# A deep fused transformer kernel: the local attention's weights and rotary tables are loaded one stage earlier, into the buffer of the preceding cross attention

## The chip, the cores and the metric

The kernel runs as one program on one core of one Trainium2 chip. Its time is the device time of one execution in microseconds (us), and the number that counts is the median of several runs. A second execution was profiled; its rows carry the same kind of times, a little longer than an unprofiled run. Engines are named as in the profile: PE is the matmul engine (PEld its weight loads), DVE, ACT and POOL are the three elementwise engines, SP issues most of the DMA transfers.

## What is computed

The input is x of 2 x 1024 tokens with 256 channels, and a context of 2 x 64 rows with 128 channels. Four blocks follow each other, each with a gated residual around it:

```python
x = x + tanh(g_xattn[0]) * L0_xattn(layernorm(x), ctx)   # causal self attention, then cross attention, each with an MLP
x = x + tanh(g_ffn[0])   * L0_ffn(layernorm(x))          # two layers: local attention, then a gated feed-forward
x = x + tanh(g_xattn[1]) * L1_xattn(layernorm(x), ctx)   # cross attention
x = x + tanh(g_ffn[1])   * L1_ffn(layernorm(x))          # router and 16 experts
```

The change is about the second block. One of its two layers, with 8 heads of 64 and windows of 128 tokens:

```python
h = shift_token(x)                       # half of the channels come from the token before
q, k, v = split(h @ wqkv)                # 256 -> 3 x 512
q, k = l2norm(q) * q_scale, l2norm(k) * k_scale
q, k = rotary_xpos(q, k)                 # tables of cos and sin by position, times a scale
x = x + softmax(mask(8 * q @ k_window.T)) @ v_window @ wo
h = layernorm(shift_token(x)) * ln_g + ln_b
a, g = split(h @ w1 + b1)
x = x + (a * gelu(g)) @ w2 + b2
```

## The kernel before, in words

The program is a chain of stages on the same core: self attention, its tail ("t1"), cross attention ("x2"), its tail ("t2"), local attention of layer 0 ("la0"), feed-forward of layer 0 ("lf0"), "la1", "lf1", cross attention "x3", router, experts and output. Tokens lie on the 128 partitions, so there are NT = 16 tiles of 128 tokens, 8 per sequence. The residual stream lives in SBUF all the time (`xres` and `x0res`), so that no stage loads its input. Every stage is a block of its own: `signals` allocates its semaphores and has a barrier over all engines in it, then each engine runs its own list of instructions written out by hand, and `release` frees the semaphores. A stage ends when every engine, SP included, is through its list; nothing of the next stage starts before.

Most stages get their weights by an "ahead" function: the stage in front gives it to its SP list, which issues the transfers at once and waits until they have landed (`sp.wait_ge(s.next_in, ahead(sp, s.next_in))`). So x2 loads what t2 needs, and la0 what lf0 needs. The local attentions are different. `local_attention(l, ahead)` issues its own six transfers at its start on SP's queue: `wqkv` (1536 KB), two small scale vectors, the cos and the sin table and `wo` (512 KB each), and only then, on the same queue, the ten transfers of the feed-forward behind it.

The other engines of local attention start like this:

- POOL clears five small regions (the last is `maskf`, L1373), each clear counted on `built1`, and then builds the masks (L1375 to L1387).
- PE waits for `w_in` (the landing of `wqkv`) and for `built1` to be 5, and then begins with `turn_x(0)`: two transposes of the first tile (L1607). ACT copies the result to `hT` (L1565), PE projects it to queries and keys in eight matmuls (`project_qk`, L1643), and ACT squares them (`norms`, L1540). DVE sums the squares (L1466), and so on through the norm, the rotation, the scores and the softmax. `turn_x` needs no weights.
- DVE waits for `tab_in` (the landing of both tables and both scale vectors), multiplies the tables in place by the scale vectors in six instructions (L1422, L1425), and only then takes part in the chain. The first reader of the tables on DVE is `cosines` (L1494), on POOL `sines` (L1406), which waits for `tab1`.

The tail t2 (`attention_tail` with finish "gate") reads the cross attention's output `ores` ([128, 8, 1024] float32) in `project1` (L846), for four groups of four tiles; the last group is read in the middle of the stage. Afterwards nothing reads `ores`, and before the change it was freed behind t2. The feed-forwards' SP list was empty, and the third cross attention had an output buffer `ores3` of its own.

Of the kernel before, what the change touches and what calls it, by code (L numbers as in the profile page):

```python
# [9 lines left out]
def build(nc, io, out):  # L10
# [21 lines left out]
    def signals(phase, names):  # L32

        sems = []
        for n in names.split():
            sems.append(nc.alloc_semaphore(f"{phase}_{n.lstrip('@')}"))
            if not n.startswith("@"):
                nc.gpsimd.sem_inc(sems[-1], 1)  # L40
        nc.all_engine_barrier()
        return namedtuple("Signals", names.replace("@", ""))(*sems)
# [7 lines left out]
    def sb(name, shape, dt=F32, where=None):  # L50
        return (where or stack).enter_context(nc.sbuf_tensor(name, shape, dt))
# [12 lines left out]
    with stack:  # L64
# [609 lines left out]
        def attention_tail(phase, weights, out_T, finish):  # L674
# [6 lines left out]
            with ExitStack() as c:  # L681
# [18 lines left out]
                s = signals(phase, "@base_done @p1_done @x1_done @stats1 @moments1 @var1 @rstd1 @z_done @z_turned @zT_done "  # L700
                            "@h_done @gelu_done @sum1 @sum2 @p3_done @y_done @gated @stats2 @moments2 @var2 @rstd2 @scaled @x_out")
                with nc.Block() as block:
                    @block.gpsimd
# [574 lines left out]
        t2ctx = ExitStack()  # L1278
        t2_weights, t2_ahead = tail_weights("t2", "L0_xattn_a2_", t2ctx, 2 * D1)
        cross_attention("x2", H1, D1, lambda t: x0res[:, t, :], ores, x2_weights, True, None, SCALE1, t2_ahead)  # L1280
        attention_tail("t2", t2_weights, lambda t, m: ores[:, t // TPB * MC + m, t % TPB * P:(t % TPB + 1) * P], "gate")
        t2ctx.close()
        x2_ctx.close()
        attn.close()

# [6 lines left out]


        def local_attention(l, ahead):
# [8 lines left out]
            with ExitStack() as c:  # L1303
                wqkv = sb(ph + "w", [P, KD, 3, INNER], F32, c)
                wo = sb(ph + "wo", [P, INNER // P, D], F32, c)
                scl = sb(ph + "scl", [P, 2, DL], F32, c)
                cosr = sb(ph + "cos", [P, TPB, 2, DL], F32, c)
                sinr = sb(ph + "sin", [P, TPB, 2, DL], F32, c)
# [25 lines left out]
                s = signals(ph, "@next_in @wo_in @w_in @tab_in @built1 @built2 @tab1 @x_turned @h_done @qk_done "  # L1334
# [20 lines left out]
                with nc.Block() as block:  # L1355
                    @block.sync
                    def _(sp):
                        sp.dma_start(wqkv[:], io["L0_ffn_wqkv"][l].rearrange("(k p) (t n) -> p k t n", p=P, t=3)).then_inc(s.w_in, 16)
                        for n, name in enumerate(["L0_ffn_q_scale", "L0_ffn_k_scale"]):
                            sp.dma_start(scl[:, n, :], rows(io[name][l])).then_inc(s.tab_in, 16)  # L1360
                        for tab, name in ((cosr, "rotary_cos"), (sinr, "rotary_sin")):
                            sp.dma_start(tab[:], io[name].rearrange("(t p) q d -> p t q d", p=P)).then_inc(s.tab_in, 16)
                        sp.dma_start(wo[:], io["L0_ffn_wo"][l].rearrange("(m p) n -> p m n", p=P)).then_inc(s.wo_in, 16)
                        sp.wait_ge(s.next_in, ahead(sp, s.next_in))
# [53 lines left out]
                    def _(dve):  # L1418

                        dve.wait_ge(s.tab_in, 64)  # L1420
# [162 lines left out]
                    def _(pe):  # L1583
                        pe.wait_ge(s.w_in, 16)
# [78 lines left out]
                        def project_out(t):  # L1663
                            pe.wait_ge(s.wo_in, 16)
                            pe.wait_ge(s.o_done, t + 1)
                            pe.wait_ge(s.h_done, min(t + LEAD_X + 1, NT))
                            for m in range(INNER // P):
                                mm = pe.matmul(bz[:, 0:D], oT[:, m * P:(m + 1) * P], wo[:, m, :],
                                               start=(m == 0), stop=(m == INNER // P - 1))
                            mm.then_inc(s.wo_done, 1)  # L1670
# [55 lines left out]
        def gated_ffn(l, weights):  # L1726
# [5 lines left out]
            with ExitStack() as c:  # L1732
# [13 lines left out]
                s = signals(ph, "@late_done @stats @moments @var_done @rstd_done @z_done @z_turned @zT_done @ag_done @gelu_done "  # L1746
                            "@h_done @base_done @p3_done @x_done @gated")

                with nc.Block() as block:
                    @block.gpsimd  # L1750
# [152 lines left out]
        for l in range(DEPTH):  # L1903
            with ExitStack() as weights_stack:
                ffn, ffn_ahead = ffn_weights(l, weights_stack)

                def next_ahead(sp, sem):

                    return ffn_ahead(sp, sem) + (x3_ahead(sp, sem) if l == DEPTH - 1 else 0)

                local_attention(l, next_ahead)
                gated_ffn(l, ffn)
# [3 lines left out]
        attn = ExitStack()  # L1916
        ores = sb("ores3", [P, B * MC3, N], F32, attn)
        E = io["L1_ffn_router_bias"].shape[0]
        wo = sb("r_wo", [P, KD, D], F32, attn)
        bo = sb("r_bo", [P, D], F32, attn)  # L1920
        nw = sb("r_nw", [P, D], F32, attn)
        SEG = P // E
        SEGW = TOK // SEG
        rw = sb("r_rw", [P, KD, 2, 2 * E], F32, attn)
        rb = sb("r_rb", [P, 1], F32, attn)
        pick = sb("r_pick", [P, 3 * P + E + 1], F32, attn)
# [550 lines left out]
        moe.close()  # L2477
        attn.close()
        x3_ctx.close()
# [67 lines left out]
```

## Time and profile before

| | us |
|---|---|
| median of 3 runs | 2176.61 (2175.91 to 2178.4) |
| the profiled execution, its own time | 2186.8 |
| its span (first to last instruction) | 2185.0 |
| stage la0, from its first DMA issue to its last residual | 987.4 to 1258.7 |
| stage la1, the same | 1413.1 to 1682.0 |

The rows of the profile name an instruction by the engine, the line of the kernel and "output<-inputs"; a timeline row gives start, duration and, in brackets, how long the engine had been idle before and what ended the idle time. "xN" is the number of instructions merged into the row, and the duration then covers all of them. "PEclk" is the share of PE's full clock that was granted. Durations of single matmuls overlap, since they are pipelined.

### The profile page before, as it was taken

The page shows a single profiled execution, that of the slowest core. Times are in us where ns is not written, and L with a number is a line of the kernel's source. Part 1 is how long each engine was busy: PE and PEld are TensorE (multiplying, and loading weights), DVE is VectorE, ACT ScalarE, POOL GpSimd, SP SyncE. Part 2 cuts the span into 40 slices and gives each one's busy share as a digit, 9 for nine tenths or more (in the row PEclk, how much of TensorE's full clock was granted, in tenths as well). Part 3 has the DMA queues.
Part 4 walks back from the last instruction along what each step waited for, and adds up shares of the span by engine and source line. Part 5 has one row for each costly group of instructions (what it writes and reads, how often), then busy time and mean ns, then how long its engine had stood idle before and what let it go on. Part 6 is the DMA issues. An engine that isn't in the chain of part 4 may idle for free. (4 is left out here: it accounts for less than half of the span.)

```text
span 2185.0 us, 32612 instructions
## 1 busy us (share of the span) xinstructions
PE 1839.2 (84%) x11580; PEld 1200.0 (55%) x11580; DVE 1276.3 (58%) x2729; ACT 1039.9 (48%) x2194; POOL 707.2 (32%) x1026
## 2 busy tenths in 40 slices
PE   6988888888899798996999889889996998862794
PEld 3455555555476465763666645456665554541694
DVE  5488888888523682325888623178885334965212
ACT  3488888888412362124776411167663111631231
POOL 0022222222323443233655411045553103450321
PEclk9999999999999899997999899989998999995897
DMA  4441111110000200003000000020000000054595
GB/s 130 135 118 40 40 40 40 40 40 1 1 0 1 59 1 1 1 0 101 1 1 1 1 0 0 31 83 1 1 1 1 0 1 15 1 185 89 164 311 144
DMA packets 99137, 99.63 MB, mean 46 GB/s; under 512 B 33740, under 2 KB 83232, under 8 KB 98848
## 3 DMA queue, kind: packets, MB, share of 16 engines
q1 hardware_dynamic: 95904, 93.21, 13.9%
q0 software_dynamic: 3072, 4.34, 1.1%
q8 instruction: 93, 1.52, 0.3%
q14 instruction: 68, 0.56, 0.1%
HBM read 80.60 MB, written 16.92 MB: 45 GB/s over the span
## 5 line engine op out<-in xcount | busy, mean ns | idle before, releaser
L577 DVE TENSOR_REDUCE negmax<-sps 128x1 f32<-128x1024 f32 x256 | 307.4, 1211 | 26.2 <-PE sps L528 26.2
L621 ACT ACTIVATE prob<-sps,negmax 128x1024 f32<-128x1024 f32 x256 | 286.5, 1119 | 9.6 <-DVE negmax L577 6.4
L537 PE MATMUL sps<-ident,prob 128*128 128x128 f32 x1152 | 177.7, 281 | 56.3 <-ACT prob L621 55.0
L537 PEld LDWEIGHTS sps<-ident,prob 128*128 128x128 f32 x1152 | 130.6, 141 | 143.8 <-ACT prob L621 129.6
L666 POOL TENSOR_TENSOR probT<-probT,after 128x128 f32<-128x128 f32 x256 | 117.1, 457 | 273.7 <-DVE probT L585 189.9
L528 PE MATMUL sps<-ks,qs 128*128 128x512 f16 x512 | 159.9, 383 | 21.7 <-DVE ores L597 18.6
L630 ACT COPY probT<-sps 128x512 f32<-128x512 f32 (+1 forms) x192 | 101.8, 530 | 17.3 <-PE sps L537 17.2
L1396 POOL TENSOR_TENSOR la0pr<-la0pr,la0ri 128x512 f32<-128x512 f32 x64 | 78.6, 1257 | 79.2 <-DVE la0ri L1435 79.2
L1396 POOL TENSOR_TENSOR la1pr<-la1pr,la1ri 128x512 f32<-128x512 f32 x64 | 78.6, 1256 | 79.0 <-DVE la1ri L1435 79.0
L1554 ACT ACTIVATE la0pr<-la0pr,la0nx 128x256 f32<-128x256 f32 x128 | 63.2, 494 | 65.1 <-DVE la0nx L1476 65.1
L1554 ACT ACTIVATE la1pr<-la1pr,la1nx 128x256 f32<-128x256 f32 x128 | 63.2, 494 | 65.0 <-DVE la1nx L1476 65.0
L585 DVE COPY probT<-sps 128x512 f32<-128x512 f32 (+3 forms) x192 | 91.3, 476 | 0.9 <-PE sps L537 0.9
L553 PE MATMUL sps<-probT,vres 128*32 128x128 f32 x2304 | 81.7, 277 | 8.5 <-POOL probT L666 5.7
L528 PEld LDWEIGHTS sps<-ks,qs 128*128 128x128 f16 x512 | 48.8, 105 | 48.7 <-issue 27.7
L2391 ACT ACTIVATE hTe<-bh,b1e 128x128 f32<-128x128 f32 x128 | 34.8, 383 | 81.9 <-PE bh L2412 81.9
L553 PEld LDWEIGHTS sps<-probT,vres 128*32 128x32 f32 x2304 | 58.2, 109 | 26.2 <-POOL probT L666 11.2
L1406 POOL TENSOR_TENSOR la0qs<-la0qn,la0sin 128x256 f32<-128x256 f32 x64 | 57.4, 931 | 44.3 <-DVE la0qn L1489 44.3
L1406 POOL TENSOR_TENSOR la1qs<-la1qn,la1sin 128x256 f32<-128x256 f32 x64 | 57.5, 929 | 43.4 <-DVE la1qn L1489 43.4
L2412 PEld LDWEIGHTS bh<-xeT,w1e 128*128 128x128 f32 x512 | 60.9, 196 | 0.7
L2412 PE MATMUL bh<-xeT,w1e 128*128 128x128 f32 x512 | 60.9, 279 | 0.0
L875 PE MATMUL t1p<-t1w,t1hT 128*128 128x256 f32 x256 | 56.6, 380 | 1.6 <-ACT t1hT L836 1.6
L875 PE MATMUL t2p<-t2w,t2hT 128*128 128x256 f32 x256 | 56.6, 380 | 1.6 <-ACT t2hT L836 1.6
(453 smaller groups left out, 4234.5 us busy)
## 6 DMA issues: line engine op xcount, KB each, us to landing
w1e<-in_fc_T SPq DMA_DIRECT2D x16, 1024.0 KB, 6.0
w2e<-in_fc_T SPq DMA_DIRECT2D x16, 1024.0 KB, 9.3
qs<-q_parts SPq DMA_DIRECT2D x128, 64.0 KB, 1.9
ks<-k_parts SPq DMA_DIRECT2D x128, 64.0 KB, 1.9
q_parts<-parts SPq DMA_DIRECT2D x8, 512.0 KB, 4.0
k_parts<-parts SPq DMA_DIRECT2D x8, 512.0 KB, 3.6
token_rows<-r_row SPq DMA_DIRECT2D x4, 544.0 KB, 3.2
mixed<-r_zero SPq DMA_DIRECT2D x1, 2056.0 KB, 11.6
```

What stands on the lines that cost most here:

```text
L528: mm = pe.matmul(slots[n % 4][:, half * 512:(half + 1) * 512], qs[:, buf, i * P:(i + 1) * P], ks[:, buf, half * 512:(half + 1) * 512], sta ...
L537: mm = pe.transpose(slots[n % 4][:, at * P:(at + 1) * P], prob[:, n % 3, t * P:(t + 1) * P], ident[:])
L553: mm = pe.matmul(acc[j * D1:(j + 1) * D1, 512:512 + P], vres[:, quad * QUAD + j, t, :], probT[:, (tile * QUAD + j) % 6, at * P:(at + 1) * ...
L577: dve.tensor_reduce(negmax[:, n % 4:n % 4 + 1], slots[n % 4][:], X, ALU.max, negate=True).then_inc(s.max_done, 1)
L621: act.activation(prob[:, n % 3, :], slots[n % 4][:], ACT.Exp, bias=negmax[:, n % 4:n % 4 + 1], accum_out=rowsum[:, tile % 2, n % QUAD:n % ...
L630: act.copy(probT[:, n % 6, lo * P:hi * P], slots[n % 4][:, lo * P:hi * P]).then_inc(s.evac_act, 1)
L666: pool.tensor_tensor(blk, blk, after[:], ALU.mult).then_inc(s.masked, 1)
L875: mm = pe.matmul(p3[j // 2][:, j % 2, :], hT[:, f, j * P:(j + 1) * P], w3[:, f, :], start=(f == 0), stop=(f == FC - 1))
L1396: ins = pool.tensor_tensor(prob[:, h:h + 2, :], prob[:, h:h + 2, :], rinv[:, h:h + 2].unsqueeze(2).to_broadcast([P, 2, 2 * P]), ALU.mult)
L1406: pool.tensor_tensor(qs[:, q * HL:(q + 1) * HL, a * 32:(a + 1) * 32], qn[:, q * HL:(q + 1) * HL, (1 - a) * 32:(2 - a) * 32], sinr[:, t % T ...
L1554: ins = act.activation(prob[:, h, :], prob[:, h, :], ACT.Exp, scale=-1.0, bias=nmax[:, h:h + 1], accum_out=rsum[:, h:h + 1])
L2412: mm = pe.matmul(bh[e % 2][:, f, :], w1e[:, e % RING, k, f * P:(f + 1) * P], xeT[:, e % 2, k * P:(k + 1) * P], start=(k == 0), stop=(k == ...
```

## The change

The six transfers of `local_attention(l)` are taken out of it and put into an ahead function, `attention_ahead(l)`. Their targets are no longer tensors of the stage but views into `ores`, which now stays allocated to the end of the kernel and also serves as the output of the third cross attention. For layer 0 the SP list of t2 issues them, after it has waited until all 16 tiles have been read by `project1`. For layer 1 the SP list of lf0 issues them at the start of that stage. Three waits go: PE's for `w_in`, DVE's for `tab_in`, and PE's for `wo_in` in `project_out`. What SP does at the start of a local attention is now only the transfers for the feed-forward (and, in layer 1, for x3). The core of the diff:

```diff
-        def attention_tail(phase, weights, out_T, finish):
+        def attention_tail(phase, weights, out_T, finish, ahead=None):
...
+                    if ahead is not None:
+                        @block.sync
+                        def _(sp):
+                            sp.wait_ge(s.p1_done, NT)
+                            sp.wait_ge(s.next_in, ahead(sp, s.next_in))
...
+        wqkv = ores[:, 0:3, :].rearrange("p a n -> p (a n)").rearrange("p (k t n) -> p k t n", k=KD, t=3)
+        wo = ores[:, 3, :].rearrange("p (m n) -> p m n", n=D)
+        cosr = ores[:, 4, :].rearrange("p (t q d) -> p t q d", q=2, d=DL)
+        sinr = ores[:, 5, :].rearrange("p (t q d) -> p t q d", q=2, d=DL)
+        scl = ores[:, 6, 0:2 * DL].rearrange("p (n d) -> p n d", n=2)
+
+        def attention_ahead(l):
+
+            def load(sp, sem):
+                sp.dma_start(wqkv, io["L0_ffn_wqkv"][l].rearrange("(k p) (t n) -> p k t n", p=P, t=3)).then_inc(sem, 16)
+                for n, name in enumerate(["L0_ffn_q_scale", "L0_ffn_k_scale"]):
+                    sp.dma_start(scl[:, n, :], rows(io[name][l])).then_inc(sem, 16)
+                for tab, name in ((cosr, "rotary_cos"), (sinr, "rotary_sin")):
+                    sp.dma_start(tab, io[name].rearrange("(t p) q d -> p t q d", p=P)).then_inc(sem, 16)
+                sp.dma_start(wo, io["L0_ffn_wo"][l].rearrange("(m p) n -> p m n", p=P)).then_inc(sem, 16)
+                return 96
+
+            return load
...
         def local_attention(l, ahead):
...
                     @block.sync
                     def _(sp):
-                        sp.dma_start(wqkv[:], ...)        # and the five others
                         sp.wait_ge(s.next_in, ahead(sp, s.next_in))
...
-                        dve.wait_ge(s.tab_in, 64)
...
-                        pe.wait_ge(s.w_in, 16)
                         pe.wait_ge(s.built1, 5)
...
-                            pe.wait_ge(s.wo_in, 16)
...
-        def gated_ffn(l, weights):
+        def gated_ffn(l, weights, ahead=None):
...
+                    if ahead is not None:
+                        @block.sync
+                        def _(sp):
+                            sp.wait_ge(s.next_in, ahead(sp, s.next_in))
...
                 local_attention(l, next_ahead)
-                gated_ffn(l, ffn)
+                gated_ffn(l, ffn, attention_ahead(l + 1) if l + 1 < DEPTH else None)
-        attn = ExitStack()
-        ores = sb("ores3", [P, B * MC3, N], F32, attn)
```

Semaphores change with it: each local attention allocates three fewer, each attention tail and each feed-forward one more.

## Rows read from the trace of the kernel before

**Rows 1.** The page's head, busy time of the engines.

```profile
span 2185.0 us, 32612 instructions
PE 1839.2 (84%) x11580; PEld 1200.0 (55%) x11580; DVE 1276.3 (58%) x2729; ACT 1039.9 (48%) x2194; POOL 707.2 (32%) x1026
```

**Rows 2.** PE's waits: line and releaser, total us, times, longest.

```profile
PE la0bz L1607 <- DMA la0w<-in_L_ffn_wqkv: 12.8, 1, 12.8
PE la1bz L1607 <- DMA la1w<-in_L_ffn_wqkv: 7.9, 1, 7.9
```

**Rows 3.** Timeline, end of t2 and start of la0: start, us, instruction.

```profile
985.84 0.73 DVE L813 TENSOR_SCALAR x0res<-xres,t2mo,t2rs 128x256 f32<-128x256 f32 x2 [1.15 <-POOL t2rs L736]
987.41 0.37 SPq L1358 DMA_DIRECT2D la0w<-in_L_ffn_wqkv  x1
...
988.67 0.53 POOL L1373 MEMSET la0mf<- 128x512 f32 x1
...
994.99 0.69 PE L1607 MATMUL la0bz<-ident,x0res 128*128 128x128 f32 x2 [12.81 <-DMA la0w<-in_L_ffn_wqkv]
...
996.62 6.19 PE L1643 MATMUL la0bs<-la0w,la0hT 128*128 128x512 f32 x8
...
1000.17 0.69 DVE L1422 TENSOR_TENSOR la0cos<-la0cos,la0scl 128x512 f32<-128x512 f32 x1 [13.59 <-DMA la0sin<-in_rotary_sin]
...
1002.05 0.75 DVE L1425 TENSOR_TENSOR la0sin<-la0sin,la0scl 128x256 f32<-128x256 f32 x2
...
1002.86 1.02 ACT L1540 ACTIVATE la0sq<-la0bs 128x1024 f32<-128x1024 f32 x1 [5.61 <-PE la0bs L1643]
...
1004.59 3.60 PE L1643 MATMUL la0bs<-la0w,la0hT 128*128 128x512 f32 x8
```

**Rows 4.** The same, end of lf0 and start of la1.

```profile
1411.65 0.69 DVE L1807 TENSOR_TENSOR x0res<-lf0p,lf0xb 128x512 f32<-128x512 f32 x1 [5.20 <-PE lf0p L1876]
1413.11 0.37 SPq L1358 DMA_DIRECT2D la1w<-in_L_ffn_wqkv  x1
...
1414.10 0.53 POOL L1373 MEMSET la1mf<- 128x512 f32 x1
...
1419.56 0.69 PE L1607 MATMUL la1bz<-ident,x0res 128*128 128x128 f32 x2 [7.94 <-DMA la1w<-in_L_ffn_wqkv]
...
1421.19 5.54 PE L1643 MATMUL la1bs<-la1w,la1hT 128*128 128x512 f32 x8
...
1426.77 1.02 ACT L1540 ACTIVATE la1sq<-la1bs 128x1024 f32<-128x1024 f32 x1 [4.96 <-PE la1bs L1643]
```

**Rows 5.** Timeline, PE's last reads of the cross attention's output in t2.

```profile
902.36 7.07 PE L846 MATMUL t2p<-t2w,ores 128*128 128x256 f32 x32
```

**Rows 6.** DMA issues: size, us from issue to landing.

```profile
la0w<-in_L_ffn_wqkv SPq DMA_DIRECT2D x1, 1536.0 KB, 7.5
...
la0wo<-in_L_ffn_wo SPq DMA_DIRECT2D x1, 512.0 KB, 10.6
```

**Rows 7.** Timeline, end of la0 and end of la1.

```profile
1248.67 3.96 PE L1597 MATMUL la0bs<-ident,la0pr 128*128 128x128 f32 x16 [3.28 <-POOL la0pr L1396]
...
1258.27 0.42 DVE L1501 TENSOR_TENSOR x0res<-la0bz,x0res 128x256 f32<-128x256 f32 x1 [2.10 <-PE la0bz L1668]
...
1681.59 0.42 DVE L1501 TENSOR_TENSOR x0res<-la1bz,x0res 128x256 f32<-128x256 f32 x1 [2.10 <-PE la1bz L1668]
```

**Rows 8.** PE by stretches: from:to, length, busy (count), granted clock, DMA.

```profile
1247.00:1248.00 1.00, 0.00 (x0) 0.80 0.00 0
1248.00:1249.00 1.00, 0.33 (x2) 0.50 0.00 0
```

**Rows 9.** POOL's scaling of probabilities, all of la0: ns min/median/max.

```profile
L1396 POOL TENSOR_TENSOR la0pr<-la0pr,la0ri x64: 1034/1037/1977, 1022.6 to 1249.6; 128x512 f32<-128x512 f32 x64
```

**Rows 10.** Timeline in la0, a DVE addition and POOL's scaling at once.

```profile
1022.50 1.23 DVE L1454 TENSOR_TENSOR la0qr<-la0qc,la0qs 128x1024 f32<-128x1024 f32 x1
...
1022.64 4.97 POOL L1396 TENSOR_TENSOR la0pr<-la0pr,la0ri 128x512 f32<-128x512 f32 x4 [3.20 <-DVE la0ri L1435]
```

More of the change, by code:

```diff
@@ L698, in attention_tail @@
                 p3 = [ps(f"{phase}p3{i}", [P, 2, D], c) for i in range(2)]
-                s = signals(phase, "@base_done @p1_done @x1_done @stats1 @moments1 @var1 @rstd1 @z_done @z_turned @zT_done "
+                s = signals(phase, "@base_done @next_in @p1_done @x1_done @stats1 @moments1 @var1 @rstd1 @z_done @z_turned @zT_done "
                             "@h_done @gelu_done @sum1 @sum2 @p3_done @y_done @gated @stats2 @moments2 @var2 @rstd2 @scaled @x_out")
                 with nc.Block() as block:
+                    if ahead is not None:
[3 more added lines that the diff above has]
+                            sp.wait_ge(s.next_in, ahead(sp, s.next_in))
                     @block.gpsimd
@@ L1276, in cross_attention @@
                 release(s)
[L1278 to L1284, printed above, removed]
         DEPTH, _, INNER3 = io["L0_ffn_wqkv"].shape
@@ L1291, in build @@
         FAR = 1e30
+        wqkv = ores[:, 0:3, :].rearrange("p a n -> p (a n)").rearrange("p (k t n) -> p k t n", k=KD, t=3)
[13 more added lines that the diff above has]
+            return load
+        t2ctx = ExitStack()
+        t2_weights, t2_ahead = tail_weights("t2", "L0_xattn_a2_", t2ctx, 2 * D1)
+        cross_attention("x2", H1, D1, lambda t: x0res[:, t, :], ores, x2_weights, True, None, SCALE1, t2_ahead)
+        attention_tail("t2", t2_weights, lambda t, m: ores[:, t // TPB * MC + m, t % TPB * P:(t % TPB + 1) * P], "gate",
+                       attention_ahead(0))
+        t2ctx.close()
+        x2_ctx.close()
         def local_attention(l, ahead):
@@ L1303, in local_attention @@
             with ExitStack() as c:
[L1304 to L1308, printed above, removed]
                 maskf = sb(ph + "mf", [P, 2, 2, P], F32, c)
@@ L1332, in local_attention @@
                 bs = ps(ph + "bs", [P, 2048], c)
-                s = signals(ph, "@next_in @wo_in @w_in @tab_in @built1 @built2 @tab1 @x_turned @h_done @qk_done "
+                s = signals(ph, "@next_in @built1 @built2 @tab1 @x_turned @h_done @qk_done "
                             "@squared @ssum_done @norm_done @clipped @rnorm_done @normed @cos_done @sin_done "
@@ L1357, in _ @@
                     def _(sp):
[L1358 to L1363, printed above, removed]
                         sp.wait_ge(s.next_in, ahead(sp, s.next_in))
@@ L1745, in gated_ffn @@
                 p3 = [ps(f"{ph}p{i}", [P, 2, D], c) for i in range(2)]
-                s = signals(ph, "@late_done @stats @moments @var_done @rstd_done @z_done @z_turned @zT_done @ag_done @gelu_done "
+                s = signals(ph, "@next_in @late_done @stats @moments @var_done @rstd_done @z_done @z_turned @zT_done @ag_done @gelu_done "
                             "@h_done @base_done @p3_done @x_done @gated")
                 with nc.Block() as block:
+                    if ahead is not None:
+                        @block.sync
+                        def _(sp):
+                            sp.wait_ge(s.next_in, ahead(sp, s.next_in))
                     @block.gpsimd
@@ L1911, in build @@
                 local_attention(l, next_ahead)
-                gated_ffn(l, ffn)
-        attn = ExitStack()
-        ores = sb("ores3", [P, B * MC3, N], F32, attn)
+                gated_ffn(l, ffn, attention_ahead(l + 1) if l + 1 < DEPTH else None)
+        r_ctx = ExitStack()
         E = io["L1_ffn_router_bias"].shape[0]
-        wo = sb("r_wo", [P, KD, D], F32, attn)
-        bo = sb("r_bo", [P, D], F32, attn)
-        nw = sb("r_nw", [P, D], F32, attn)
+        wo = sb("r_wo", [P, KD, D], F32, r_ctx)
+        bo = sb("r_bo", [P, D], F32, r_ctx)
+        nw = sb("r_nw", [P, D], F32, r_ctx)
         SEG = P // E
         SEGW = TOK // SEG
-        rw = sb("r_rw", [P, KD, 2, 2 * E], F32, attn)
-        rb = sb("r_rb", [P, 1], F32, attn)
-        pick = sb("r_pick", [P, 3 * P + E + 1], F32, attn)
+        rw = sb("r_rw", [P, KD, 2, 2 * E], F32, r_ctx)
+        rb = sb("r_rb", [P, 1], F32, r_ctx)
+        pick = sb("r_pick", [P, 3 * P + E + 1], F32, r_ctx)
         def router_ahead(sp, sem):
@@ L2477, in build @@
         moe.close()
+        r_ctx.close()
+        x3_ctx.close()
         attn.close()
-        x3_ctx.close()
 def shape_constants(tokens=1024, dim=64, window=128):
```

## The prediction

> **What bounds the kernel now.** I first read the page's head: PE is busy for 1839 of 2185 us, DVE for 1276 and ACT for 1040 [rows 1]. No engine is busy all the time, so the share alone prices nothing, and the chain of waits on the page only covers the output at the very end. The change touches two places, the starts of the local attentions, so the second view was PE's waits by releaser. There are two waits of PE for a weight transfer in the whole list: the first instruction of la0 ended a wait of 12.8 us, the first of la1 one of 7.9 us, and both name the landing of `wqkv` [rows 2]. Neither figure is the possible gain, since part of each idle time is the end of the stage before, where DVE and POOL still finish the last tiles.
>
> The third view was therefore the timeline around each start. In la0 the last residual of t2 ends at 985.84 + 0.73 = 986.57, the first instructions of the new stage stand at 987.41, `wqkv` takes 7.5 us to land, and PE begins at 994.99 [rows 3, 6]. In that time no other engine does anything that takes long: POOL's fifth clear ends at 988.67 + 0.53 = 989.20, and DVE stands still until 1000.17 because the tables land later still [rows 3]. In la1 the stage before ends at 1411.65 + 0.69 = 1412.34, the start is at 1413.11, the fifth clear ends at 1414.63 and PE begins at 1419.56 [rows 4]. What the reader is to see: from PE's first transpose on, each stage is one chain (transpose, copy, eight projections, squares, sum, norm, and so on). The squares on ACT had waited for PE in both layers (5.61 and 4.96 us, released by L1643), so the chain starts with PE, and PE starts with the transfer. Everything behind it, to the end of the kernel, moves with it, because stages are separated by barriers.
>
> **The change part by part.**
>
> *PE's wait for `w_in` goes.* The next thing PE waits for is `built1`, the five clears of POOL. They don't depend on any transfer. PE then starts at 989.20 in la0 instead of 994.99, which is 5.8 us earlier, and at 1414.63 instead of 1419.56 in la1, on the old time scale, which is 4.9 us earlier [rows 3, 4]. Together 10.7 us.
>
> *DVE's wait for `tab_in` goes.* The tables' six instructions run from 1000.17 to 1002.80, so 2.6 us [rows 3]. Before, they ended ahead of the first sum of squares, which needs the end of the first square, 1002.86 + 1.02 = 1003.88. Now they can run from about 987.4 to 990.0, while the chain, moved by 5.8 us, needs DVE at about 998.1. They stay hidden, behind PE's first projections, and 8 us are to spare. They are worth nothing in the sum. Without that cover they would cost 2.6 us per layer. But they now run at the same time as POOL's clears, which they never did before; see the next point but one.
>
> *The wait for `wo_in` goes.* `wo` landed 10.6 us after its issue, at 1001.6 if the issue is put at 990.96, its place behind the five others; it is first used for tile 0, after its whole softmax. Nothing waited for it: PE's waits in the list name no such transfer. Worth nothing.
>
> *Where the clears and the tables meet.* The nearest row is POOL's scaling in the loop, which reads and writes SBUF: 1034 ns at least, 1977 ns at most [rows 9]. The row of a group in which DVE adds two tensors from SBUF at the same time shows how: four scalings take 4.97 us instead of 4 x 1.03 = 4.14 [rows 10], so one of them was held for some 0.8 to 0.94 us, about as long as the rest of DVE's 1.23 us. If clears are held in the same way, the worst case is that they wait for the tables' whole 2.6 us; the best is 0. I take 0, because a clear reads nothing, while every row with a hold is one of a POOL instruction that reads. The sum is 10.7 with 0 and 10.7 - 2 x 2.6 = 5.5 with the whole hold. The Trainium skill, SBUF — State Buffer, "Who interferes with whom", says that a DVE instruction with two SBUF inputs gets in the way of a GpSimd instruction that reads SBUF, and not of one that only writes it. By that rule the result is the 10.7, by the held rows alone the 5.5; no row of this trace has a clear beside such a DVE instruction, so it doesn't decide between them.
>
> *PE's clock.* The first eight projections take 6.19 us in la0 and 5.54 us in la1, the next eight in la0 take 3.60 [rows 3, 4]: the first ones run partly at half the clock, 1.2 instead of 2.4 GHz, after PE has stood still. After the change PE's idle time in front is 12.8 - 5.8 = 7.0 us in la0 and 7.94 - 4.9 = 3.0 in la1. The nearest row is the end of la0: PE was idle for 3.28 us before 1248.67 [rows 7], and within that time the granted clock went from full to half (0.80 in the microsecond from 1247, 0.50 in the next) [rows 8]. So I expect the clock to be low again at both starts and charge nothing. The bounds: if it stayed high, the first eight would take 3.60 us, which gives 2.6 us in la0 and 1.9 us in la1. If it stayed low through all eight, they would take up to twice 3.60 = 7.2, so 1.0 and 1.7 us would be lost.
>
> *The transfers at their new place.* For layer 0, SP waits until `project1` has read all 16 tiles. The last of its 32 matmuls ends at 902.36 + 7.07 = 909.4 [rows 5]. Six issues and the landing of the last took from 987.41 to about 1001.6, so 14.2 us [rows 3, 6]; they are through at 924, and the stage ends at 986.57. So 62 us are to spare, covered by t2's second half. SP's list was empty there, so nothing is queued behind the wait but SP's own end of the stage. For layer 1, they start with lf0 at about 1259 and are through at 1273, with 139 us to spare before 1412.34 [rows 4, 7]. In both places the engines' work reads other tensors. Cost 0; the upper bound would be PE's matmuls getting slower beside the traffic, but in la0 eight projections took 3.60 us from 1004.59, while the feed-forward's weights were coming in, just what their number of 0.45 us each says of full clock.
>
> *The feed-forward's transfers* stand behind six fewer issues on SP's queue, and go out at 987.4 instead of 996.7. Nothing reads them before lf0. Worth nothing.
>
> *Semaphores.* Three fewer in each local attention, one more in four other stages. The step from the last instruction of a stage to the first of the next is 0.84 us into la0 and 0.77 us into la1 [rows 3, 4], with the same number of names in the new stage and quite different numbers in the old one (23 and 15), so a name more or less is worth well under 0.1 us. I take 0, with 0.1 either way.
>
> **Does the rest of the stage keep its length?** From the first square to the end of the last residual, la0 takes 1258.69 - 1002.86 = 255.8 us and la1 takes 1682.01 - 1426.77 = 255.2 us [rows 3, 4, 7]. The two starts differ in clock and timing and end within 0.6 us of each other, so a start that moves as a whole should carry through.
>
> **The sum.** 5.8 + 4.9 = 10.7 us. The span goes from 2185.0 to 2174.3, the profiled execution's own time, 1.8 us above its span, from 2186.8 to 2176.1. The median of the runs lies 10.2 us below the profiled one, and both differences are kept: 2176.6 - 10.7 = 2165.9 us. Its own range is 2164.7 to 2168.6: 1.2 less for the 0.6 us above in each layer, 2.7 more for a clock that stays low through the first eight projections of both.
>
> **The rivals.**
>
> *The clears are held by the tables* (price above): the gain is 5.5 and the time 2171.1. For it speaks that POOL and DVE do hold each other [rows 9, 10] and that they now start in the same microsecond. Against it, that clears don't read.
>
> *The clock stays high at the start of la1*, where PE only rests 3.0 us: 1.9 us more, 2164.0. At la0 as well: 2161.4. For it speaks that 3.0 is less than the 3.28 of [rows 7]; against it that the clock there fell well before those 3.28 us were over [rows 8].
>
> *The change does not do what it says*, and the start of the local attention waits as before: SP is not through with the transfers when t2 ends, so the barrier holds all engines. That needs transfers 62 us later than they have ever been here. Then 2176.6.
>
> *Slower.* In the loop of local attention, POOL's scaling releases PE's transposes (L1597 waits for it [rows 7]), and one scaling of four is held by DVE in each tile: the group of four takes 4.97 us [rows 10]. If the new start moved POOL and DVE against each other so that a second one is held in each of the 2 x 16 tiles, that would cost 32 x 0.94 = 30 us, and the time would be 2196. It decides from 12 further holds (10.7 / 0.94). Against it speaks that la0 and la1, with different starts, have the same length.
>
> **How the numbers follow.** The forecast has 0.64, the clears 0.13, the high clock 0.13, no effect 0.06, the holds 0.04. A difference of 0.2%, which is 4.4 us, is about what a measurement of this kernel can tell from none. Faster by more: 0.64 + 0.13 + 0.13 = 0.90. Within it: 0.06. Slower: 0.04. The range runs from the high clock (2164.0, and some way towards 2161.4) to the held clears (2171.1): 2162.8 to 2171.4.
>
> **What the profile of the changed kernel would show.** PE's waits no longer name a transfer at L1607 of either layer; the releaser is the clear of `maskf` on POOL, and PE's first transpose starts 1.8 and 1.5 us after the stage's first instruction, not 7.6 and 6.4. The six table instructions stand in the first 3 us of the stage. The three large clears still take 0.53 us each. SP's issues of the six transfers stand at about 909.5 and at the start of lf0. The stretch from the first square to the last residual stays at 255 to 256 us. The prediction is wrong if the clears take longer or start later, if PE's first eight projections take over 7 us, or if the stretch in the loop grows.

## The result, and the profile after

| | us |
|---|---|
| kernel before, median of 12 | 2178.49 (2175.49 to 2187.02) |
| changed kernel, median of 12 | 2172.86 (2169.48 to 2182.51) |
| ratio | 0.9971, 95% interval 0.9959 to 0.9982 |
| profiled execution of the changed kernel, and its span | 2177.25, 2175.5 |

The kernel became faster, as forecast, but by about 6.3 us (0.29%, from the ratio) where 10.7 were forecast. The measured 2172.86 lies 1.5 us above the upper end of the range. The changed kernel was measured twice more, below: 0.9960 and 0.9957. Weighted by their intervals the three give 0.9965 (0.9957 to 0.9972), which is 7.7 us.

The page's head, to be compared with [rows 1]:

```profile
span 2175.5 us, 32612 instructions
PE 1846.6 (85%) x11580; PEld 1204.5 (55%) x11580; DVE 1277.6 (59%) x2729; ACT 1039.7 (48%) x2194; POOL 706.5 (32%) x1026
```

The same number of instructions, and the same work. PE's waits (line and releaser, total us, times, longest), where [rows 2] stood:

```profile
PE la0bz L1618 <- POOL la0mf L1386: 7.1, 1, 7.1
PE la1bz L1618 <- POOL la1mf L1386: 3.1, 1, 3.1
```

Both waits for the transfer are gone, and what ends the idle time now is POOL's fifth clear: 7.1 and 3.1 us, where 7.0 and 3.0 were forecast. The timeline of the start of la0, against [rows 3]:

```profile
994.35 0.37 SPq L1720 DMA_DIRECT2D lf0w<-in_L_ffn_w  x1
...
994.39 0.69 DVE L1434 TENSOR_TENSOR ores<-ores 128x512 f32<-128x512 f32 x1 [0.88 <-PEq L41]
994.70 0.52 POOL L1384 MEMSET la0kT<- 128x512 f32 x1 [0.21 <-issue]
...
995.16 0.53 POOL L1385 MEMSET la0v<- 128x512 f32 x1
...
995.62 0.52 POOL L1386 MEMSET la0mf<- 128x512 f32 x1
...
996.20 0.69 PE L1618 MATMUL la0bz<-ident,x0res 128*128 128x128 f32 x2 [7.08 <-POOL la0mf L1386]
...
996.28 0.84 DVE L1437 TENSOR_TENSOR ores<-ores 128x256 f32<-128x256 f32 x2
996.36 0.48 POOL L1389 TENSOR_SCALAR_AFFINE_SELECT la0mf<-la0mf 128x128 f32<-128x128 f32 x1
...
997.83 5.78 PE L1654 MATMUL la0bs<-ores,la0hT 128*128 128x512 f32 x8
...
1003.65 1.02 ACT L1552 ACTIVATE la0sq<-la0bs 128x1024 f32<-128x1024 f32 x1 [5.20 <-PE la0bs L1654]
```

and of la1, against [rows 4]:

```profile
1413.55 0.53 POOL L1384 MEMSET la1kT<- 128x512 f32 x1
...
1414.47 0.52 POOL L1386 MEMSET la1mf<- 128x512 f32 x1
...
1415.05 0.56 PE L1618 MATMUL la1bz<-ident,x0res 128*128 128x128 f32 x2 [3.07 <-POOL la1mf L1386]
...
1415.41 0.94 DVE L1437 TENSOR_TENSOR ores<-ores 128x256 f32<-128x256 f32 x2
...
1416.56 4.64 PE L1654 MATMUL la1bs<-ores,la1hT 128*128 128x512 f32 x8
...
1421.23 1.02 ACT L1552 ACTIVATE la1sq<-la1bs 128x1024 f32<-128x1024 f32 x1 [4.06 <-PE la1bs L1654]
```

PE starts 1.85 us after the stage's first instruction in la0 (996.20 - 994.35) and 1.56 us in la1. The reader is to see three things. DVE multiplies the tables while POOL clears, and the clears take 0.52 to 0.53 us as before. The masks' affine select, which reads SBUF, took 0.48 us here beside DVE's products, and DVE's last pair of products 0.84 and 0.94 us instead of 0.75 [rows 3]. And the eight projections took 5.78 us in la0, 4.64 in la1: the clock was low for a part of them again. The issues of the six transfers (SP's timeline) stand in the middle of t2 and at the start of lf0, and nothing waits for them:

```profile
916.40 0.37 SPq L1300 DMA_DIRECT2D ores<-in_L_ffn_wqkv  x1
...
919.25 5.80 SPq L1305 DMA_DIRECT2D ores<-in_L_ffn_wo  x1
```

Where the time went is read from the lengths of the stages (from the first instruction of one to that of the next, worked out from the timelines):

```
profile                self attention   la0     la1     the other stages, to the end of the experts
before                     462.5       272.3   269.9      1059.2
before, second             468.9       267.2   267.2      1057.8
changed                    468.6       265.7   261.1      1058.8
changed, second            469.5       265.4   261.1      1056.8
changed, third             462.1       265.5   261.1      1065.6
```

The third profile of the changed kernel ran in another place than the others, which is why its other stages are longer (below). The first profile of before had both local attentions at the long end, 7.8 us longer in sum than the second. Against the second, the changed kernel gains 1.6 us in la0 and 6.1 in la1; against the first, 6.7 and 8.8. The self attention runs long ahead of the change: it takes from 462 to 469.5 us, at the short and at the long end in either kernel.

### The profile page after: what moved, and what is told of

It is laid out like the page before. It is cut to its first block and busy times, and to the rows that moved or that the text cites. A ratio compares the mean times of both kernels' runs of the same rounds, so it can differ in the third digit from the quotient of the medians.

```text
span 2175.5 us, 32612 instructions
## 1 busy us (share of the span) xinstructions
PE 1846.6 (85%) x11580; PEld 1204.5 (55%) x11580; DVE 1277.6 (59%) x2729; ACT 1039.7 (48%) x2194; POOL 706.5 (32%) x1026
## 5 line engine op out<-in xcount | busy, mean ns | idle before, releaser
L621 ACT ACTIVATE prob<-sps,negmax 128x1024 f32<-128x1024 f32 x256 | 286.2, 1118 | 10.2 <-DVE negmax L577 6.8
L537 PE MATMUL sps<-ident,prob 128*128 128x128 f32 x1152 | 182.1, 287 | 55.6 <-ACT prob L621 54.7
L553 PEld LDWEIGHTS sps<-probT,vres 128*32 128x32 f32 x2304 | 58.3, 110 | 26.5 <-POOL probT L666 11.2
L1419 POOL TENSOR_TENSOR la0qs<-la0qn,ores 128x256 f32<-128x256 f32 x64 | 57.3, 925 | 37.6 <-DVE la0qn L1501 37.6
L1419 POOL TENSOR_TENSOR la1qs<-la1qn,ores 128x256 f32<-128x256 f32 x64 | 57.3, 925 | 37.0 <-DVE la1qn L1501 37.0
```

The source lines that it names most:

```text
L537: mm = pe.transpose(slots[n % 4][:, at * P:(at + 1) * P], prob[:, n % 3, t * P:(t + 1) * P], ident[:])
L553: mm = pe.matmul(acc[j * D1:(j + 1) * D1, 512:512 + P], vres[:, quad * QUAD + j, t, :], probT[:, (tile * QUAD + j) % 6, at * P:(at + 1) * ...
L621: act.activation(prob[:, n % 3, :], slots[n % 4][:], ACT.Exp, bias=negmax[:, n % 4:n % 4 + 1], accum_out=rowsum[:, tile % 2, n % QUAD:n % ...
L1419: pool.tensor_tensor(qs[:, q * HL:(q + 1) * HL, a * 32:(a + 1) * 32], qn[:, q * HL:(q + 1) * HL, (1 - a) * 32:(2 - a) * 32], sinr[:, t % T ...
```

## The experiments

Kernels of one batch ran on one chip with the kernel before (medians 2180.04, 2190.15 and 2191.88 us in the three). The second and the third ran in other places, where the stage of the experts took 146 to 147 instead of 137 us; ratios hold within a batch.

### First batch: is the kernel before steady, and is each layer worth its part?

**before_again** is the kernel before, **after_again** the changed one, both unaltered.

> The kernel before, unchanged, timed against itself and profiled once more. Theory A (chance): the change saves 10 to 11 us in every execution, and the medians moved by only 5.6 because executions differ in the stages in front of the change (self attention took 461.2 us in the profile before and 467.3 in the profile after). Then self attention in this profile may take anything from 461 to 468 us. Rival B (given back in front): self attention is always some 461 us in this program and always some 467 in the changed one. Both expect la0 at 272 and la1 at 270 us from stage start to stage start, and a ratio to itself of 1.000, with single executions up to 10 us apart.

> The changed kernel, unchanged, timed and profiled once more. Theory A: the ratio comes out between 0.9950 and 0.9965 with new runs, and self attention in the profile is anywhere from 461 to 468 us. Rival B: ratio 0.997 again, self attention 467 us again. Rival C (given back behind): self attention like that of the kernel before, but local attention stages longer than in the first profile of the changed kernel (265.7 and 261.1 us), since those had a lucky clock; 267 and 265 us by the prediction's 5.8 and 4.9.

Measured: before_again 2181.52 us, 1.0000 (0.9988 to 1.0013); after_again 2173.98 us, 0.9960 (0.9946 to 0.9974). The profile of before_again was expected by both theories to have la0 at 272 and la1 at 270 us; it had both at 267.2. The kernel before has the same median but starts otherwise in this profile (timeline of before_again, start of la0; the stage begins at 994.6):

```profile
1001.22 0.69 PE L1607 MATMUL la0bz<-ident,x0res 128*128 128x128 f32 x2 [11.83 <-DMA la0w<-in_L_ffn_wqkv]
...
1002.86 5.07 PE L1643 MATMUL la0bs<-la0w,la0hT 128*128 128x512 f32 x8
...
1007.97 1.02 ACT L1540 ACTIVATE la0sq<-la0bs 128x1024 f32<-128x1024 f32 x1 [4.49 <-PE la0bs L1643]
...
1008.68 0.75 DVE L1425 TENSOR_TENSOR la0sin<-la0sin,la0scl 128x256 f32<-128x256 f32 x2
1009.46 1.22 DVE L1466 TENSOR_REDUCE la0ss<-la0sq 128x16 f32<-128x1024 f32 x1
```

The transfer landed a microsecond earlier (6.6 us against 7.5), the projections took 1.1 us less, and then the tables, which I had called hidden, were in the way: the sum of squares starts 1.49 us after the square where it otherwise starts 1.13 after it.

**only_l0** and **only_l1** move the transfers of one layer alone; the other layer's go into the same place in `ores`, but are issued and waited for in its own stage:

```diff
+    if l == own:            # own = 1 in only_l0, 0 in only_l1
+        sp.dma_start(wqkv, ...).then_inc(s.w_in, 16)      # and the five others
+    if l == own: dve.wait_ge(s.tab_in, 64)
+    if l == own: pe.wait_ge(s.w_in, 16)
+    if l == own: pe.wait_ge(s.wo_in, 16)
```

> Only layer 0's six transfers are moved into the tail before; layer 1 issues its own at its start as before, into the same buffer. Theory A: 5.8 us faster than before (ratio 0.9973), la0 266 us, la1 270 us. Rival B: 5.8 less what is given back in front (6 us if it comes with any change of the program): ratio 1.000. Rival C: la0 266 us in the profile and a smaller gain than 5.8 in the times.

> Only layer 1's six transfers are moved, into the feed-forward of layer 0; layer 0 issues its own at its start. Theory A: 4.9 us faster than before (ratio 0.9977), up to 1.9 more when the clock is high for part of the first projections; la0 272 us, la1 261 to 265 us. Rival B: ratio 1.000. Rival C: la1 in the profile at 263 to 265 us and no gain from the clock, so 0.998.

Measured: only_l0 2177.17 us, 0.9988 (0.9973 to 1.0003); only_l1 2179.56 us, 0.9993 (0.9981 to 1.0006). Alone they are inconclusive: both intervals hold "no effect", and the sum, 4.1 us, is less than the 8.7 of after_again beside them, though within what the intervals allow. Their profiles say more, together with those of the other runs of both kernels (us from the stage's start; "sum" is the start of DVE's first sum of squares, where the start is over and the loop sets the pace; "rest" goes from there to the start of the next stage):

```
               la0: transpose  projections  sum   rest     la1: transpose  projections  sum   rest
not moved
 before               7.58        6.19     16.58  255.7           6.45        5.54     14.79  255.1
 before_again         6.59        5.07     14.83  252.3           6.43        5.16     14.92  252.3
 only_l1 / only_l0    6.59        5.12     15.30  254.2           6.55        5.47     14.83  252.9
moved
 changed              1.85        5.78     10.43  255.2           1.56        4.64      8.87  252.2
 after_again          1.85        5.66     10.31  255.1           1.56        4.63      8.88  252.2
 only_l0 / only_l1    1.85        5.67     10.32  255.2           1.57        6.17     10.54  255.6
 after_third          1.85        5.71     10.35  255.1           1.56        4.63      8.88  252.2
```

The column "sum" gives what the change removes. Averages: la0 15.57 to 10.35, la1 14.85 to 9.29. That is 5.2 and 5.6 us, together 10.8, near the 10.7 of the prediction. The column "rest" is the surprise: the same instructions take 252 to 253 or 254 to 256 us, in both kernels. Only_l1 gained nearly nothing in la1 because it drew 6.17 and 255.6.

### What the two lengths are

The steps of the loop from one last addition to the next are the same in all profiles until the last two tiles. There no further projections are left for PE, and it waits for POOL's scaling. Timeline of PE in the changed kernel, the last tile but one, first la0 (three rows), then la1 (three rows):

```profile
1233.42 1.15 PE L1608 MATMUL la0bs<-ident,la0pr 128*128 128x128 f32 x8 [4.21 <-POOL la0pr L1409]
...
1237.17 1.91 PE L1626 MATMUL la0bqk<-ident,la0qr 128*128 128x128 f32 x8
1239.02 2.99 PE L1637 MATMUL la0bv<-la0pT,la0v 128*64 128x128 f32 x32
...
1650.91 3.68 PE L1608 MATMUL la1bs<-ident,la1pr 128*128 128x128 f32 x16 [4.21 <-POOL la1pr L1409]
1654.42 1.04 PE L1626 MATMUL la1bqk<-ident,la1qr 128*128 128x128 f32 x8
1655.39 1.97 PE L1637 MATMUL la1bv<-la1pT,la1v 128*64 128x128 f32 x32
```

The last two kinds take 1.91 and 2.99 us in la0, 1.04 and 1.97 in la1. The windows (from:to, length, PE busy, granted clock, DMA) show why:

```profile
1233.00:1234.00 1.00, 0.58 (x5) 1.00 0.00 0
1234.00:1235.00 1.00, 0.57 (x5) 0.66 0.00 0
1235.00:1236.00 1.00, 0.59 (x3) 0.50 0.00 0
...
1240.00:1241.00 1.00, 1.00 (x14) 0.50 0.00 0
1241.00:1242.00 1.00, 1.00 (x18) 0.93 0.00 0
...
1650.00:1651.00 1.00, 0.09 (x1) 0.87 0.00 0
1651.00:1652.00 1.00, 1.00 (x5) 0.50 0.00 0
...
1653.00:1654.00 1.00, 1.00 (x5) 0.50 0.00 0
1654.00:1655.00 1.00, 1.00 (x11) 0.92 0.00 0
```

Both times PE had rested 4.2 us. In la1 the clock fell to half just before PE resumed and was back 3.4 us later. In la0 it fell only after PE had resumed, and stayed at half for 6.8 us. The step of this tile is 16.64 us in la0 and 14.51 in la1; that of the last one, which in the kernel before stood behind a wait of 3.28 us [rows 7], 9.86 and 9.05. Together 2.9 us, and the "rest" columns differ by 3.0. If this is the cause, the difference must go when PE does not rest there.

### Second batch: PE kept busy at the end, and PE started earlier

**busy_ends_before** (the kernel before) and **busy_ends_after** (the changed one) give PE seven additional matmuls ahead of the transposes of each of the last two tiles. Nobody reads what they write.

```diff
+    if it >= NT - 2:
+        pe.wait_ge(s.normed, NT)
+        for _n in range(7):
+            pe.matmul(bqk[:, 0:INNER], ident[:], wqkv[:, 0, 0, :], start=True, stop=True)
     turn_probs(it)
```

> The kernel before, with seven matmuls whose result nobody reads in front of the probability transposes of each of the last two tiles of both local attentions, where PE stands still for 4.2 and 3.3 us. Theory D (the length of a local attention behind its start depends on where PE's clock falls and rises again in its last two tiles): from the first sum of squares to the next stage both layers take 251 to 252.5 us, never 254 to 256; the median falls by 2 to 4 us. Rival E (the two lengths come from how POOL and DVE hold each other, or from chance in other places): both lengths, 252 and 255, are seen as before, or both grow by what the seven matmuls take beyond the gap, and the median stays or rises.

> The changed kernel with the same seven matmuls in the last two tiles. Theory D: layer 0, which ended in the long form in all three looks with its transfers moved (255.2 us), takes 251 to 252.5 us behind its first sum of squares, as layer 1 does; the time is 2 to 4 us below the changed kernel's, and below the busy-ended kernel before by 4.5 + 4.9 to 5.8, so 9 to 11 us, since then only the starts differ. Rival E: no gain over the changed kernel, and the difference to the busy-ended kernel before stays at 6 to 8 us.

Measured: busy_ends_before 2191.72 us, 1.0014 (1.0000 to 1.0029); busy_ends_after 2181.81 us, 0.9963 (0.9950 to 0.9977). The medians are 9.9 us apart, by the ratios it is 11.2. From the first sum on, the four stages take 253.2, 253.2, 253.2 and 253.3 us: the spread of 252 to 256 is gone, as theory D says, but its 251 to 252.5 us and its fall of the median by 2 to 4 us are missed. The stages' lengths are 268.3 and 268.2 before, 263.7 and 263.6 after, so 9.3 us between the two kernels, all of it in the starts (la1 drew a slow one in busy_ends_after, 10.3 us until the first sum). Timeline and windows of busy_ends_after at the same place as above:

```profile
1236.91 6.17 PE L1695 MATMUL la0bqk<-ores,ident 128*128 128x512 f32 x14
1242.92 1.91 PE L1608 MATMUL la0bs<-ident,la0pr 128*128 128x128 f32 x16
1245.27 1.97 PE L1637 MATMUL la0bv<-la0pT,la0v 128*64 128x128 f32 x32 [0.44 <-DVE la0pT L1451]
...
1243.00:1244.00 1.00, 1.00 (x11) 1.00 0.00 0
...
1246.00:1247.00 1.00, 1.00 (x24) 1.00 0.00 0
```

The clock stays at 1.00 and the products take 1.97 us. But seven matmuls are too many: each stands as two instructions, 14 in 6.17 us, longer than the wait that they fill, so PE is now late by itself, and the ends come out between the two lengths.

**pe_first** goes at the next wait in the chain. The first transposes need none of the clears, so the changed kernel's PE now waits for them where it first could clash with them: for the first two, in `hT`, ahead of the projections, and for those of `kT`, `v` and the masks' region ahead of the scores:

```diff
-    pe.wait_ge(s.built1, 5)
     # project_qk(t)
+    if t == 0: pe.wait_ge(s.built1, 2)
     # score(t)
+    if t == 0: pe.wait_ge(s.built1, 5)
```

**all_three** is pe_first with the seven matmuls of above and nine more behind the last real ones of t2, to keep the clock up into la0.

> The changed kernel with PE's wait for the clears moved: two clears before the first projections, all five before the first scores, none before the first transposes. Theory A (the start of the stage is a chain that hangs on PE's first instruction): PE starts 0.1 us after the stage instead of 1.8 and 1.5, so the stages start up to 3.2 us earlier in sum, ratio to the kernel before 0.9955 to 0.994. Rival F (the tables on DVE or the clock are what is late next): the first sum of squares stays where it is, at 8.9 to 10.4 us behind the start, and the time stays the changed kernel's.

> The changed kernel with PE starting first, the seven matmuls in the last two tiles, and nine such matmuls behind the last real one of the tail in front of layer 0, so that PE is busy up to that stage's end. Theory D with A: the first eight projections of layer 0 take 3.6 to 4.5 us instead of 5.7, its first sum of squares stands at 6.5 to 7.5 us instead of 10.3, both layers take 251 to 252.5 us behind it; in all 8 to 11 us less than the changed kernel, ratio to the kernel before 0.991 to 0.993. Rival E with F: ratio 0.995 to 0.997.

Measured: pe_first 2177.83 us, 0.9945 (0.9926 to 0.9964); all_three 2177.16 us, 0.9944 (0.9923 to 0.9965). In pe_first PE begins 0.04 us after the first instruction of la0 (timeline):

```profile
993.30 0.37 SPq L1722 DMA_DIRECT2D lf0w<-in_L_ffn_w  x1
...
993.34 0.66 PE L1617 MATMUL la0bz<-ident,x0res 128*128 128x128 f32 x2 [5.28 <-PEq L41]
...
999.85 1.02 ACT L1552 ACTIVATE la0sq<-la0bs 128x1024 f32<-128x1024 f32 x1 [4.28 <-PE la0bs L1655]
```

Its local attentions take 260.1 and 260.2 us, 5.4 and 0.9 less than those of the changed kernel: the earlier start (10.3 to 7.7 and 8.9 to 7.6 us until the first sum), and in la0 the short rest, 252.4 instead of 255.2. In all_three the nine matmuls did keep the clock up (the first projections take 3.60 us), but t2 itself took 153.7 instead of 150.4 us, and what was won at the start was paid there. Its ratio missed the expected 0.991 to 0.993.

### Third batch: the fillers cut to the gap

**after_third** is the changed kernel again. **short_ends** is busy_ends_after with four and three matmuls instead of seven (`range(4 if it == NT - 2 else 3)`). **pe_first_again** repeats pe_first. **short_fill** is pe_first with these four and three, and four behind t2 instead of nine.

> The changed kernel once more, on the chip of the three others of this batch. The starts of la0 and la1 gave 5.1 and 5.2 us on average in the looks so far (first sum of squares 10.4 and 9.7 us behind the stage's start against 15.5 and 14.9), and the stage ends took between 252.2 and 255.6 us in either kernel. Theory D: ratio to the kernel before 0.9950 to 0.9970, and one more look at which ends it draws; layer 0 again in the long form of 255.2 if its start fixes it.

> The changed kernel with four and three matmuls for PE in the last two tiles instead of seven each. Seven took 6.2 us of PE (14 instructions) where the gaps are 4.2 and 3.3 us, so they kept the clock up and gave it back in length, 253.2 us each time. Theory D: four and three take 3.5 and 2.6 us, fit, and both layers take 251.0 to 252.0 us behind the first sum of squares; the time is 2 to 4 us below the changed kernel's. Rival E: 252 to 255 as without them.

> PE first, unchanged, beside the changed kernel on one chip. Its profile had the first sum of squares at 7.7 and 7.6 us, against 8.9 to 10.5 with the wait. Theory A: 2.5 to 4 us below the changed kernel, stage lengths 260 to 263 us. Rival F: no difference to the changed kernel.

> PE first, four and three matmuls in the last two tiles, and four (3.5 us, before: nine, which took 7.9 us and made the tail 3.3 us longer) behind the last real one of t2, where PE stands still for 4.4 us. Theories A and D: t2 at 150.4 us again, la0 first sum of squares at 6 to 7.7 us, both layers 251 to 252 us behind it, so stages of 257 to 260 us; 6 to 8 us below the changed kernel, ratio to the kernel before 0.991 to 0.9935. Rival E with F: no lower than PE first.

Measured:

```
after_third      2181.22 us   0.9957 (0.9940 to 0.9975)   rest 255.1 and 252.2
short_ends       2178.42 us   0.9943 (0.9927 to 0.9959)   rest 251.1 and 251.1
pe_first_again   2175.10 us   0.9923 (0.9904 to 0.9942)   rest 252.5 and 252.6
short_fill       2172.55 us   0.9912 (0.9896 to 0.9927)   rest 251.0 and 251.2
```

With a filler that fits, all four ends take 251.0 to 251.2 us, 1 us under the short length. Short_ends alone can't be told from after_third by the times (the intervals overlap); its gain is read from the stages. Short_fill is faster than both kernels: 19.3 us below the kernel before and 8.7 below the changed one. In it t2 keeps its 150.4 us, and PE's waits for `built1` at the starts are gone. PE around the boundary in short_fill (timeline):

```profile
981.61 3.60 PE L898 MATMUL t2tps<-t2w,ident 128*128 128x512 f32 x8
...
987.05 0.41 PE L1620 MATMUL la0bz<-ident,x0res 128*128 128x128 f32 x2 [1.85 <-PEq L41]
```

## Why the prediction was right in direction and off in size

*PE's wait for `w_in` goes; `built1` takes its place.* Right, in place and size: PE starts 1.85 and 1.56 us into the stage, released by the fifth clear. Over the profiles of the table of starts the start until the first sum is 10.8 us shorter, against 10.7; in the pair with seven fillers it is 9.3. One caution: the 7.5 us landing of [rows 6], on which the 5.8 us of la0 rest, was a long one. In before_again and only_l1 it took 6.6, in busy_ends_before 7.7. What la0 lost against my number (5.2 us against 5.8), la1 won (5.6 against 4.9), in part by a higher clock.

*The tables are hidden.* True of the changed kernel. Before it they weren't quite: in the quicker starts they held the sum back by 0.4 to 0.8 us.

*The clears beside the tables.* Right, and the rival with 5.5 us falls: they took 0.52 to 0.53 us beside DVE, while the first affine select took 0.48 and 0.43 us, against 0.30 and 0.29 before. By the Trainium skill, SBUF — State Buffer, "Who interferes with whom", a GpSimd instruction that only writes is not in the way of a DVE instruction with two SBUF inputs, one that reads is. The trace agrees with both halves. The held ones lie beside PE's work and cost nothing.

*PE's clock at the start.* The direction was right (low again, 5.66 to 5.78 us for la0's first eight). In la1 it was back earlier in three of four profiles, 4.64 us: a gain of 0.9, within the bound of 1.9 that I gave. In the fourth, only_l1, it took 6.17.

*The transfers, `wo`, the feed-forward's transfers, the semaphores.* Nothing waits for any of them. The other stages have the same lengths, except those that differ between two profiles of one kernel as well.

*"Does the rest of the stage keep its length?"* This is the step that failed. I took two stages of one execution that agreed within 0.6 us as proof of a fixed length and put 0.6 per layer into my own range. Both had drawn the long end. The length is 252 to 253 or 254 to 256 us, by where the clock falls around PE's waits of 4.2 and 3.3 us in the last two tiles. In la0, with the transfers not moved, it was 255.7, 252.3 and 254.2, and with the start moved it was 255.1 to 255.2 in four profiles of four. Where before had drawn the short end, as in before_again, 2.8 us of the gain are given back there. The stretch from the first square to the last residual, which was to stay at 255 to 256 us, was 255.4 in la0 of the changed kernel and 252.4 in la1.

How much that is on average hangs on what the kernel before usually draws, and the profiles alone don't say: their means give a gain of 10.0 us (10.8 from the starts, less 1.1 in la0, plus 0.3 in la1). The times say more. The next table sets the lengths of both local attentions in each profile against before_again's 534.4 us, and beside it stands what the times gave against the kernel before (us, from the ratios, with their intervals):

```
                   both stages   534.4 less that   by the times
changed               526.6            7.8          7.7  (6.0 to 9.4), three measurements
only_l0               533.3            1.1          2.6  (-0.7 to 5.9)
only_l1               535.7           -1.3          1.5  (-1.3 to 4.1)
busy_ends_before      536.6           -2.2         -3.1  (-6.4 to 0)
busy_ends_after       527.3            7.1          8.1  (5.0 to 11.0)
short_ends            521.4           13.0         12.5  (9.0 to 16.0)
pe_first              520.3           14.1         12.0  (7.9 to 16.2)
pe_first_again        520.6           13.8         16.9  (12.7 to 21.0)
short_fill            517.4           17.0         19.3  (16.0 to 22.8)
```

All nine lie within the intervals, only_l1 at the edge of its own; all_three, whose t2 is 3.3 us longer, fits too (519.9 us, so 11.2 with that taken off, against 12.3). Set against the 542.1 us of the first profile, on which the prediction rests, every row would be 7.8 us higher and outside its interval; against the mean of the profiles, 537.9, four of the nine would lie outside. So the usual length of the kernel before is near that of before_again, and the account of the change closes on it: the starts give 4.5 us in la0 and 6.0 in la1, la0's rest takes 2.8 back, la1's rest keeps its 252.3, together 7.7 us as measured. This is inferred from one profile a kernel; no run shows how often each length is drawn.

*The base.* My sum started from 2176.61, the median of 3 runs; 12 and 30 runs of the same kernel gave 2178.49 and 2180.04. Single executions of it lay between 2175.09 and 2187.02 us in these 42, and the self attention stage alone moves by 7 us. With the base of the result's own runs, the same 10.7 us give 2167.8. Of the 7.0 us between forecast and result, then, 1.9 come from the base, and 5.1 from the gain, which by the medians there was 5.6 and not 10.7. The base alone is more than the 1.5 us by which the result lies above the range: part of the miss is bad luck with three runs. The sign was there before, though. The profiled execution took 2186.8 us, 10.2 more than the median, and I kept that difference as if profiled executions were always longer. They are not: those of the other runs lie on both sides of their medians (2175.64 against 2177.17 in only_l0, 2177.34 against 2181.22 in after_third). Only one of the 42 executions was longer than 2186.8, and 7.8 of the 10.2 us are the two local attentions at their long ends.

What stays open: why la0 always drew the long end once its start was moved. That it hangs on the start's place is likely, since pe_first, which starts 1.8 us earlier still, drew the short end in la0 in both of its profiles, but no run shifted the start in small steps.

*The rivals.* The high clock from the first projection on did not come (4.64 us at the least, against 3.60). The transfers weren't late. The held clears did not come either; the measured 6.3 us are near that rival's 5.5 by chance. Nor did further holds of POOL's scaling: the steps of the loop are the same, and with the fillers the rest of the stage is equal in both kernels to 0.1 us.

## What to carry to other kernels

When a start of a stage is moved, look at what the stage does at its end: where PE rests a few microseconds between short bursts, the same instructions can take 3 us more or less, and one profile shows only one draw. A profiled execution far above the median of the others is a warning: find the stages in which it is longer before pricing a change in them. Take at least two profiles of the kernel before as the base for a gain under 0.5%, and don't take the agreement of two stages in one of them for a law. A wait that has taken another's place (here the clears) is the next thing to remove: letting PE begin before the clears and filling its rests, with matmuls cut to the gap and not beyond it, gave 8.7 us more by the medians.

## What was not expected of the hardware

- After a rest of PE of the same 4.2 us, the granted clock was at half for 3.4 us or for 6.8 us, depending on whether it had fallen just before PE resumed or about a microsecond after. The Trainium skill, TensorE: Matmul & The Clock Gate, "HAM oscillation — how this bites in real kernels", describes such a clock that falls in PE's waits; here the late fall costs 3 us in a stage of 260, and with the waits filled the stage is never that long.
- A matmul of 512 columns in float32 stands as two instructions, 14 of them in 6.17 us, so 0.44 us each at full clock.
- The landing of the same 1.5 MB differed in la0: it took 7.5 and 7.7 us in two profiles (before, busy_ends_before) and 6.6 in two others (before_again, only_l1). In la1 it took 6.4 in all three profiles of before, before_again and busy_ends_before.
